# First batch of an attention and expert kernel: split loads, another order of jobs, and unread products in the pauses

## The chip, the cores and the metric

One core of a Trainium2 chip runs the program. The metric is the device time of one execution in microseconds (us). TensorE, VectorE, ScalarE, GpSimd and SyncE are the core's engines; they share the on-chip memory, and order between them comes from semaphores. TensorE's clock has two levels, 2.4 GHz (a granted clock of 1.00 in the tables) and 1.2 GHz (0.50).

## The reference

For 4 sequences of 1024 tokens of width 256: attention with 16 heads of 16, then a top-2 mixture of 8 experts, each followed by a residual and a layernorm.

```python
q = einsum('bsc,oc->bso', x, wq); k = ...wk; v = ...wv          # 16 heads of 16
q_embed = stack([softplus(q) * cos(pos), softplus(q) * sin(pos)])
k_embed = stack([softplus(k) * cos(pos + bias), softplus(k) * sin(pos + bias)])
attn = softmax(q_embed @ k_embed.T / 4); x = layernorm(x + (attn @ v) @ wo.T)
gates = softmax(x @ router_w + router_b); top 2, capacity 640 tokens an expert
h = gelu(rows_e @ w1[e] + b1[e]); out = h @ w2[e] + b2[e]
x = layernorm(x + sum over the chosen experts of gate * out)
```

## The kernel before, in words

The program has two launches in one: `attention`, then `experts`, with a turn between them at which the engines meet.

**Attention.** The work is cut into 16 groups (4 sequences, 4 groups of 4 heads), each of 16 steps; a step is one tile of 128 keys against 512 queries for 4 heads. TensorE makes a step's scores (`scores`, L828), ScalarE their exponentials (L621), and TensorE one step later the product with the values (`values`, L852). Queries and keys enter in two parts, a rounded one and its remainder, so that three products stand for one precise one.

Between the steps TensorE runs *jobs* from a table written by hand (`misc_schedule`). A job belongs to a step; negative steps are those before the attention of the first group. For batch 0, the first eight heads of the first sequence, they are four projections `qk` (query and key, first and second half of the sequence: units 0 to 3), four jobs of values `v`, `norms` (a bound on the scores, from squares) and `count`. The jobs before step 0 write to four PSUM banks in turn, `misc` and the first halves of the three score buffers (`banks`, `bank`), and a job waits until the bank that it takes has been read. TensorE waits at step 0 until all early jobs are read (`s_free`), for the first half of the stacks (`s_half`), and then reads a flag that `count` gives, to choose between two forms of the group (`choose`).

A projection's unit runs through the engines. ScalarE makes a softplus in three passes (`softplus`, L581 to L585). VectorE (`split_unit`) makes `raw` (L978), multiplies by the angles' cosines and sines into `emb` (L988) and rounds it (L994); GpSimd subtracts for the remainder (`split_rest`, L496). ScalarE squares `raw` for the norms (L590). SyncE stores both parts in DRAM (`store`, L330) and loads them back as stacks in the layout of the heads (`fill_half`, L369, half of the sequence each; `fill`, L384, for the next group). Step 4 of the first group waits for the second half. Each engine's own order is the order of its program: VectorE makes the keys' angles (`key_angles`) ahead of unit 0, and the constants (`set_up`, L958 to L966) between units 1 and 2.

**The turn.** After the last group VectorE finds the slots of the last tokens (L1175), GpSimd scatters their rows to the experts' buffers in DRAM (L511), and the launch ends. The second launch loads the rows (L1347), turns them on TensorE (L1403), and runs expert after expert: hidden layer L1423, output L1442.

## Time and profile before

| | |
|---|---|
| median of three runs | 1006.29 us (1005.87 to 1007.37) |
| the profiled execution, its own time | 1010.19 us |
| its span in the trace | 1008.4 us |
| TensorE busy (weight loads apart) | 907.8 us, 90% |
| weight loads | 518.8 us, 51% |
| VectorE, ScalarE, GpSimd busy | 631.4, 657.1, 362.0 us |

The trace gives every instruction's start and duration from the start of the span. An idle time stands before the instruction that ends it, with the operation that released it behind an arrow. An f32 product of TensorE is two records, so that a projection of two products counts x4 and a job of values x8.

### The profile page before, as it was taken

How to read it: one execution, taken by the hardware profiler on the slowest of the kernel's cores; microseconds unless marked ns; L12 is line 12 of the kernel's file. 1: busy time of each engine (PE TensorE's matmuls, PEld its weight loads, DVE VectorE, ACT ScalarE, POOL GpSimd, SP SyncE). 2: the span in 40 equal slices, each digit the busy share in tenths (PEclk: the TensorE clock that was granted, in tenths of full speed). 3: DMA queues.
4: the chain of work that ended last, by engine and by line, in shares of the span. 5: the costliest groups of instructions: out<-in, count | busy, mean ns of one | idle time of the engine just before them, and what ended most of it. 6: DMA issues, size and time to landing. Idle time of an engine off the chain costs nothing. (4 is left out here: it accounts for less than half of the span.)

```text
span 1008.4 us, 19281 instructions
## 1 busy us (share of the span) xinstructions
PE 907.8 (90%) x7597; PEld 518.8 (51%) x7597; DVE 631.4 (63%) x1109; ACT 657.1 (65%) x762; POOL 362.0 (36%) x271
## 2 busy tenths in 40 slices
PE   5599999999999999999999989999099999999950
PEld 2333343334344334444434434344089999999940
DVE  5467556647868465767564775437466777877626
ACT  4289888897778888867888777986134344444315
POOL 2137243433235654415545520233603333222332
PEclk9599999999999999999999999999589999999985
DMA  6728742333415343332542425231165544333245
GB/s 225 256 79 266 264 147 75 131 137 131 173 49 179 118 169 142 131 133 89 192 143 66 174 73 187 67 101 35 50 199 137 137 111 131 91 97 95 27 114 246
DMA packets 62133, 135.32 MB, mean 134 GB/s; under 512 B 8563, under 2 KB 33460, under 8 KB 60752
## 3 DMA queue, kind: packets, MB, share of 16 engines
q1 hardware_dynamic: 42848, 85.99, 25.6%
q0 software_dynamic: 19184, 47.99, 15.9%
q8 instruction: 62, 1.02, 0.4%
q14 instruction: 39, 0.32, 0.1%
HBM read 72.47 MB, written 61.95 MB: 133 GB/s over the span
## 5 line engine op out<-in xcount | busy, mean ns | idle before, releaser
L621 ACT ACTIVATE prob<-spsum 128x1024 f32<-128x1024 f32 x512 | 492.8, 1022 | 136.7 <-PE spsum L828 130.2
L852 PE MATMUL opsum<-prob,val 128*17 128x512 f32 x2048 | 270.5, 598 | 2.6 <-DVE oraw L1187 1.4
L828 PE MATMUL spsum<-area_q 32*128 32x512 f32 x1536 | 136.0, 429 | 4.7 <-issue 2.4
L828 PEld LDWEIGHTS spsum<-area_q 32*128 32x128 f32 x1536 | 75.4, 185 | 117.1 <-issue 72.5
L1380 POOL DMA_INDIRECT sum_scratch<-eo,add_idx x40 | 70.3, 1757 | 176.3 <-ACT eo L1483 169.2
L828 PE MATMUL spsum<-stacks 32*128 32x512 f32 x1536 | 132.0, 425 | 1.2 <-ACT prob L621 0.5
L828 PEld LDWEIGHTS spsum<-stacks 32*128 32x128 f32 x1536 | 72.4, 183 | 113.9 <-ACT prob L621 61.8
L494 POOL TENSOR_TENSOR square<-raw 128x512 bf16<-128x512 f32 x28 | 58.0, 2073 | 192.6 <-DVE raw L983 192.6
L1194 DVE RECIPROCAL oden<-oden 128x256 f32<-128x256 f32 x62 | 108.7, 1753 | 2.1
L496 POOL TENSOR_TENSOR area_s<-emb,area_s 128x1024 fp32r<-128x1024 f32 x32 | 76.0, 2376 | 41.9 <-DVE area_s L994 41.9
L537 POOL TENSOR_TENSOR onorm<-oraw,oden 128x512 f32<-128x512 f32 x31 | 42.2, 1361 | 131.7 <-DVE oden L1194 131.7
L1472 ACT ACTIVATE hraw<-hp,b 128x640 f32<-128x640 f32 x64 | 51.0, 797 | 56.5 <-PE hp L1423 56.5
L511 POOL DMA_INDIRECT dispatched<-res,scatter_idx x64 | 65.5, 1023 | 58.9 <-issue 25.1
L852 PEld LDWEIGHTS opsum<-prob,val 128*17 128x17 f32 x2048 | 36.4, 95 | 95.2 <-ACT prob L621 60.2
L1483 ACT ACTIVATE eo<-biased,gate 128x256 f32<-128x256 f32 x40 | 20.4, 510 | 88.9 <-DVE biased L1590 88.9
L1187 DVE COPY oraw<-opsum 128x512 f32<-128x512 f32 x31 | 21.4, 692 | 77.2 <-PE opsum L852 68.9
L665 PE MATMUL misc<-xT,wqkv 128*128 128x512 f32 x116 | 60.5, 646 | 8.0 <-DMA wqkv<-in_wk 7.4
L1442 PE MATMUL yp<-area_q,hid 128*128 128x256 f32 x480 | 61.1, 284 | 0.0
L1442 PE MATMUL yp<-w2s,hid 128*128 128x256 f32 x480 | 59.8, 282 | 0.0
L1423 PE MATMUL hp<-xe,area_s 128*128 128x320 f32 x384 | 59.3, 315 | 0.0
L1423 PEld LDWEIGHTS hp<-xe,area_s 128*128 128x128 f32 x384 | 58.6, 194 | 0.0
L1442 PEld LDWEIGHTS yp<-area_q,hid 128*128 128x128 f32 x480 | 57.8, 189 | 0.1
(198 smaller groups left out, 1075.5 us busy)
## 6 DMA issues: line engine op xcount, KB each, us to landing
split_scratch<-area_s POOLq DMA_DIRECT2D x56, 512.0 KB, 4.1
area_k<-in_w SPq DMA_DIRECT2D x16, 1024.0 KB, 5.8
stacks<-split_scratch SPq DMA_DIRECT2D x28, 512.0 KB, 5.5
area_q<-split_scratch SPq DMA_DIRECT2D x28, 512.0 KB, 5.4
dispatched<-blank POOLq DMA_DIRECT2D x1, 5300.0 KB, 25.7
rows<-dispatched SPq DMA_DIRECT2D x7, 662.5 KB, 4.6
xT<-in_xT SPq DMA_DIRECT2D x4, 1024.0 KB, 6.6
res<-in_x SPq DMA_DIRECT2D x4, 1024.0 KB, 8.4
```

The lines of the kernel that those rows point to most:

```text
L494: pool.tensor_tensor(square[:, i], raw[:], raw[:], ALU.mult).then_inc(s_square, 1)
L496: pool.tensor_tensor(split[u % 2][:, 1], embs[u % 2][:], split[u % 2][:, 0].bitcast(F32), ALU.subtract).then_inc(s_split, 1)
L511: pool.indirect_dma_start(disp_d, bass.IndirectOffsetOnAxis(ap=scatter_idx[:, k, t:t + 1], axis=0), ress[UNITS[u][0] % 2][:, t, :], None, ...
L621: act.activation(prob[u % NPB][:], spsum[u % NSB][:].rearrange("p a n -> p (a n)"), ACT.Exp, scale=HD ** -0.5).then_inc(s_exp, 1)
L665: ins = pe.matmul(misc[:], wqkv[:, qk, k, P * ct:P * (ct + 1)], xT[:, k, HALF * half:HALF * (half + 1)], start=k == 0, stop=k == KC - 1)
L828: ins = pe.matmul(spsum[u % NSB][:, j % 2, :], kst[par][rows, a, P * kt:P * (kt + 1)], qst[par][rows, b, cols], start=i == 0, stop=i == 2 ...
L852: ins = pe.matmul(opsum[32 * j:32 * j + HD + 1, :], val[b % 2][:, kt, h0 + j, :], prob[(2 * s + j // 2) % NPB][:, HALF * (j % 2):HALF * (j ...
L1194: tell(dve.reciprocal(half, half), s_sums)
L1380: pool.indirect_dma_start(sum_d, bass.IndirectOffsetOnAxis(ap=add_idx[e % 2][:, t:t + 1], axis=0), eo[e % 2][:, t, :], None, bounds_check= ...
L1423: ins = pe.matmul(hp[n % 2][:, h, 0:CH], w1s[e % 2][:, b, k, P * m:P * (m + 1)], xe[e % 2][:, a, k, CH * h:CH * (h + 1)], start=k == 0 and ...
L1442: ins = pe.matmul(yp[n % 2][:, 0:DIM], hids[:, a, m, P * t:P * (t + 1)], w2s[e % 2][:, b, m, :], start=m == 0 and i == 0, stop=m == HK - 1 ...
L1472: act.activation(hraw[n % NH][:].rearrange("p (h n) -> p h n", h=2), hp[n % 2][:, :, 0:CH], ACT.Gelu, bias=b1[:, e, m:m + 1]).then_inc(s_g ...
```

## The change

It touches the first batch, and adds products in pauses of TensorE.

- The loads of x and of the query angles come in halves, each with a semaphore; the constants come in another order, `blank` later.
- The early jobs are ordered qk, v, norms, count, and use seven banks in place of four.
- `raw` of units 2 and 3 goes to the buffers `oden` and `onorm`. VectorE makes the remainders of batch 0 itself; GpSimd doesn't take part in batch 0's units, and sets up the constants.
- The keys' angles are made for the first half only at first. For the second half ScalarE makes the first products, and VectorE adds the second (`late_angles`), around the readouts of norms and count. The values are copied by ScalarE (`first_values`), which also rounds units 2 and 3.
- `idle_products`: products of a constant with itself, 128x128, to a bank that nobody reads afterwards: 14 at the start; 14 when two squares are there and 4 when three are, ahead of the norms; 12 ahead of step 0; 36 when the last slots are known; 8 at the start of the second launch.

```diff
-        put(-14 + i, ("qk", 0, i))
-        put((-8, -7, -4, -3)[i], ("v", 0, i))
+        put(-10 + i, ("qk", 0, i))
+        put(-6 + i, ("v", 0, i))
         put((1, 5, 9, 13)[i], ("qk", 1, i))
-    put(-6, ("norms", 0))
-    put(-5, ("count", 0))
+    put(-2, ("norms", 0))
+    put(-1, ("count", 0))
...
-        banks = [misc, *(b[:, 0, :] for b in spsum)]
+        banks = [misc, *(b[:, n, :] for b in spsum for n in range(2))]
...
-            sp.dma_start(wqkv[:, 0], wq_d).then_inc(s_wqk, 16)
-            sp.dma_start(xT, xT_d[0]).then_inc(s_xT, 16)
-            sp.dma_start(wqkv[:, 1], wk_d).then_inc(s_wqk, 16)
-            sp.dma_start(qtrig, trig_d).then_inc(s_trig, 16)
-            sp.dma_start(blank[:], blank_d).then_inc(s_blank, 16)
+            sp.dma_start(wqkv[:, 0], wq_d).then_inc(s_wqk[0], 16)
+            sp.dma_start(xT[:, :, 0:HALF], xT_d[0][:, :, 0:HALF]).then_inc(s_xfirst[0], 16)
+            sp.dma_start(wqkv[:, 1], wk_d).then_inc(s_wqk[1], 16)
+            sp.dma_start(qtrig[:, :, 0:HALF], trig_d[:, :, 0:HALF]).then_inc(s_trig[0], 16)
+            sp.dma_start(xT[:, :, HALF:], xT_d[0][:, :, HALF:]).then_inc(s_xfirst[1], 16)
+            sp.dma_start(qtrig[:, :, HALF:], trig_d[:, :, HALF:]).then_inc(s_trig[1], 16)
             sp.dma_start(wqkv[:, 2], wv_d).then_inc(s_wv, 16)
+            sp.dma_start(tri_f[:], tri_d).then_inc(s_const, 16)
+            sp.dma_start(blocks_f[:], blocks_d).then_inc(s_const, 16)
+            sp.dma_start(ident[:], ident_d).then_inc(s_const, 16)
             sp.dma_start(woT[:, :, 0:DIM], wo_d).then_inc(s_const, 16)
...
+            sp.dma_start(blank[:], blank_d).then_inc(s_blank, 16)
...
+            for i in range(2):
+                pool.memset(val[i][:, :, :, HD:HD + 1], 1.0)
+            pool.memset(ones[:], 1.0)
+            pool.memset(before[:], 0.0)
+            pool.memset(unit[:], 0.0).then_inc(s_clear, 1)
+            pool.wait_ge(s_clear, 1)
+            pool.wait_ge(s_const, 16 * NCONST)
+            pool.tensor_copy(tri[:], tri_f[:])
+            for k in range(KC):
+                pool.tensor_copy(unit[:, k, P * k:P * (k + 1)], ident[:])
+            pool.tensor_copy(blocks[:], blocks_f[:]).then_inc(s_setup, 1)
...
+            def first_batch():
+
+                softplus(0)
+                softplus(1)
+                first_square(0)
+                softplus(2)
+                first_square(1)
+                softplus(3)
+                first_values(0)
+                first_square(2)
+                first_square(3)
+                act.wait_ge(s_trig[1], 16)
+                for t in range(2):
+                    act.mul(ktrig[:, 0, t, HALF:], qtrig[:, 1 - t, HALF:], ang[:, (3, 5)[t], 0:1]).then_inc(s_late, 1)
+                for i in range(1, 4):
+                    first_values(i)
+                for u in (2, 3):
+                    act.wait_ge(s_emb, u - 1)
+                    for v in (u - 2,):
+                        stored(act, 0, v)
+                    act.copy(split[u % 2][:, 0], embs[u % 2][:]).then_inc(s_hi, 1)
...
                     pe.wait_ge(s_setup, 1)
+                    if c == 0:
+                        for u, count in ((2, 14), (3, 4)):
+                            pe.wait_ge(s_square, u)
+                            idle_products(pe, misc[:, 0:P], ident, count)
                     pe.wait_ge(s_square, 4 * c + 4)
...
+            pe.wait_ge(s_krow, 1)
+            idle_products(pe, spsum[2][:, 1, 0:P], row_ones[:].bitcast(F32), 14)
             for s in range(first, last + 1):
                 if s == 0:
 
+                    idle_products(pe, bank(("norms", 0))[:, 0:P], ident, 12)
                     pe.wait_ge(s_free, early)
...
+            pe.wait_ge(s_idx, 2 * len(UNITS))
+            idle_products(pe, spsum[1][:, 0, 0:P], ident, 36)
             pe.br("attention_done")
...
+            def first_product(u):
+
+                qk, half = u % 2, u // 2
+                table = ktrig[:, 0] if qk else qtrig
+                tell(dve.tensor_tensor(embs[u % 2][:], raw_of(u)[:].unsqueeze(1).to_broadcast((P, 2, HALF)),
+                                       table[:, :, HALF * half:HALF * (half + 1)], ALU.mult), s_emb)
+
+            def first_rest(u):
+
+                dve.wait_ge(s_hi, u + 1)
+                counts[s_hi.name] = u + 1
+                tell(dve.tensor_tensor(split[u % 2][:, 1], embs[u % 2][:], split[u % 2][:, 0].bitcast(F32),
+                                       ALU.subtract), s_split)
+
+            def late_angles(t):
+
+                dve.wait_ge(s_late, t + 1)
+                link(dve.scalar_tensor_tensor(ktrig[:, 0, t, HALF:], qtrig[:, t, HALF:], ang[:, 4, 0:1],
+                                              ktrig[:, 0, t, HALF:], ALU.mult, ALU.add))
+
+            def first_split(u):
+
+                split_parts(0, u)
+                tell(dve.tensor_tensor(split[u % 2][:, 1], embs[u % 2][:], split[u % 2][:, 0].bitcast(F32),
+                                       ALU.subtract), s_split)
+
+            def first_batch():
+
+                dve.wait_ge(s_trig[0], 16)
+                key_angles(0, slice(0, HALF))
+                for u in (0, 1):
+                    first_raw(u)
+                    first_split(u)
+                for u in (2, 3):
+                    first_raw(u)
+                dve.wait_ge(s_trig[1], 16)
+                first_product(2)
+                read_out(("norms", 0))
+                late_angles(0)
+                read_out(("count", 0))
+                dve.wait_ge(s_vcopy, 4)
+                dve.sem_inc(s_free, 4)
+                counts[s_free.name] += 4
+                late_angles(1)
+                first_product(3)
+                for u in (2, 3):
+                    first_rest(u)
+                dve.wait_ge(s_setup, 1)
...
+def idle_products(pe, bank, square, count):
+
+    for _ in range(count):
+        pe.matmul(bank, square[:], square[:], start=True, stop=True)
...
+            idle_products(pe, yp[1][:, 0:P], ident, 8)
```

TensorE's program at its start, before (spsum and misc are the banks; square, tops: norms and count):

```order
L665 MATMUL misc<-xT,wqkv 128x512 x2
L665 MATMUL spsum<-xT,wqkv 128x512 x6
L674 MATMUL misc<-wqkv,xT 128x256 x4
L674 MATMUL spsum<-wqkv,xT 128x256 x4
L681 MATMUL spsum<-square,blocks 32x512 x4
L686 MATMUL spsum<-ident,tops 1x128
L674 MATMUL misc<-wqkv,xT 128x256 x4
L674 MATMUL spsum<-wqkv,xT 128x256 x4
```

And in the changed kernel (L1348 are the unread products):

```order
L1348 MATMUL spsum<-row_ones 128x128 x14
L716 MATMUL misc<-xT,wqkv 128x512 x2
L716 MATMUL spsum<-xT,wqkv 128x512 x6
L725 MATMUL spsum<-wqkv,xT 128x256 x12
L725 MATMUL misc<-wqkv,xT 128x256 x4
L1348 MATMUL spsum<-ident 128x128 x18
L736 MATMUL spsum<-square,blocks 32x512 x4
L741 MATMUL spsum<-ident,tops 1x128
L1348 MATMUL spsum<-ident 128x128 x12
```

All four value jobs stand ahead of the norms, and unread products stand in three places.

VectorE's program in the first batch, from the product of unit 1 on, before (area_s: rounded part, or with emb as input the remainder; oden, onorm: raw of units 2 and 3 in the change; area_k: the keys' angles):

```order
L988 TENSOR_TENSOR emb<-raw,area_k 128x1024
L994 CAST area_s<-emb 128x1024
...
L978 SCALAR_TENSOR_TENSOR raw<-spsum,soft 128x512
L988 TENSOR_TENSOR emb<-raw,qtrig 128x1024
L994 CAST area_s<-emb 128x1024
L978 SCALAR_TENSOR_TENSOR raw<-spsum,soft 128x512
L988 TENSOR_TENSOR emb<-raw,area_k 128x1024
L994 CAST area_s<-emb 128x1024
L1012 COPY val<-misc 128x32x16
L1012 COPY val<-spsum 128x32x16
L1015 TENSOR_REDUCE tops<-spsum 128x1
```

And in the changed kernel:

```order
L1086 TENSOR_TENSOR emb<-raw,area_k 128x1024
L1092 CAST area_s<-emb 128x1024
L1043 TENSOR_TENSOR area_s<-emb,area_s 128x1024
L1015 SCALAR_TENSOR_TENSOR oden<-spsum,soft 128x512
L1015 SCALAR_TENSOR_TENSOR onorm<-spsum,soft 128x512
L1024 TENSOR_TENSOR emb<-oden,qtrig 128x1024
L1111 TENSOR_REDUCE tops<-spsum 128x1
L1112 MEMSET pairs 1x128
L1037 SCALAR_TENSOR_TENSOR area_k<-qtrig,ang,area_k 128x512
...
L1037 SCALAR_TENSOR_TENSOR area_k<-qtrig,ang,area_k 128x512
L1024 TENSOR_TENSOR emb<-onorm,area_k 128x1024
L1031 TENSOR_TENSOR area_s<-emb,area_s 128x1024 x2
```

The constants and the copies of values have left; four remainders and two halves of the angles have come, and the second product of each pair stands behind the readouts of norms and count.

## Rows read from the trace of the kernel before

**Rows 1.** The page, part 2: granted TensorE clock in 40 slices of 25.2 us.
```profile
PEclk9599999999999999999999999999589999999985
```

**Rows 2.** The chain of waits, in order of time: start, us, what.
```profile
735.44 16.20 PE hp L1423 x96
...
766.90 14.07 PE hp L1423 x96
```

**Rows 3.** Timeline, TensorE: start, us, operation, count of records, idle before.
```profile
7.43 3.78 PE L665 MATMUL misc<-xT,wqkv 128*128 128x512 f32 x4 [7.43 <-DMA wqkv<-in_wk]
...
18.87 1.89 PE L674 MATMUL spsum<-wqkv,xT 128*128 128x256 f32 x8
...
35.04 3.78 PE L674 MATMUL misc<-wqkv,xT 128*128 128x256 f32 x8
...
38.62 2.73 PE L674 MATMUL spsum<-wqkv,xT 128*128 128x256 f32 x8
...
43.75 2.07 PE L828 MATMUL spsum<-area_q 32*128 32x512 f32 x14 [2.40 <-issue]
...
56.16 0.97 PE L828 MATMUL spsum<-area_q 32*128 32x512 f32 x12
...
59.15 1.98 PE L665 MATMUL misc<-xT,wqkv 128*128 128x512 f32 x4
```

**Rows 4.** Timeline, VectorE, first 45 us.
```profile
15.44 1.23 DVE L988 TENSOR_TENSOR emb<-raw,qtrig 128x1024 f32<-128x1024 f32 x1
...
16.70 0.69 DVE L994 CAST area_s<-emb 128x1024 fp32r<-128x1024 f32 x1
...
18.26 2.73 DVE L988 TENSOR_TENSOR emb<-raw,area_k 128x1024 f32<-128x1024 f32 x1
...
36.20 0.14 DVE L1023 TENSOR_SCALAR flags<-pairs 1x1 int32<-1x1 f32 x1
...
41.86 0.69 DVE L1012 COPY val<-spsum 128x512 f32<-128x512 f32 x1 [2.24 <-PE spsum L674]
```

**Rows 5.** Timeline, ScalarE, one pass of the first softplus.
```profile
11.87 0.63 ACT L584 ACTIVATE soft<-soft 128x512 f32<-128x512 f32 x1
```

**Rows 6.** Timeline, GpSimd, remainders of units 0, 1 and 3.
```profile
17.55 2.36 POOL L496 TENSOR_TENSOR area_s<-emb,area_s 128x1024 fp32r<-128x1024 f32 x1 [16.60 <-DVE area_s L994]
...
21.86 2.35 POOL L496 TENSOR_TENSOR area_s<-emb,area_s 128x1024 fp32r<-128x1024 f32 x1 [1.95 <-DVE area_s L994]
...
32.35 2.34 POOL L496 TENSOR_TENSOR area_s<-emb,area_s 128x1024 fp32r<-128x1024 f32 x1 [1.95 <-DVE area_s L994]
```

**Rows 7.** SyncE's loads of the stacks, and landing of loads into area_q.
```profile
28.79 1.76 SPq L369 DMA_DIRECT2D area_q<-split_scratch  x4
...
41.28 1.75 SPq L369 DMA_DIRECT2D area_q<-split_scratch  x4
...
DMA to landing us min/median/max: 2.8/3.9/6.0
```

**Rows 8.** Windows of half a us; the column 1.00 to 0.50 is the granted clock.
```profile
23.00:23.50 0.50, 0.00 (x0) 0.00 (x0) 0.47 (x1) 0.00 (x0) 0.50 (x1) 0.73 1.03 389
...
40.00:40.50 0.50, 0.50 (x3) 0.42 (x2) 0.00 (x0) 0.00 (x0) 0.00 (x0) 0.70 0.40 156
...
43.50:44.00 0.50, 0.25 (x4) 0.28 (x8) 0.00 (x0) 0.00 (x0) 0.00 (x0) 0.71 0.75 262
```

**Rows 9.** Timeline, TensorE, products of 8 columns with f32 weights.
```profile
275.23 1.06 PE L732 MATMUL misc<-wr,x1T 128*128 128x8 f32 x8
```

**Rows 10.** Timelines at the turn of the launches: VectorE, GpSimd, ScalarE, TensorE.
```profile
715.23 0.19 DVE L1175 TENSOR_REDUCE scatter_idx<-rt 128x4 int32<-128x32 f32 x1
...
726.49 0.97 POOL L511 DMA_INDIRECT dispatched<-res,scatter_idx  x1 [0.30 <-issue]
...
729.17 1.28 ACT L1463 ACT_TABLE_LOAD   x1 [17.61 <-PEq L159]
...
731.30 1.25 PE L1403 MATMUL tp<-ident,rows 128*128 128x128 f32 x4 [18.17 <-DMA rows<-dispatched]
```

More of the change, by code:

```diff
@@ L273, in jobs_at, with raw_of @@
             return jobs.get(s, ())
+        def raw_of(u):
+            return (oden, onorm)[u - 2] if u in (2, 3) else raws[u % 2]
         def softplus_at(s):
@@ L490, in split_rest @@
                 pool.wait_ge(s_raw, u + 1)
-                if c:
-                    pool.wait_ge(s_full, number["norms", c - 1] + 1)
-                if c:
-                    pool.tensor_tensor(square[:, i], raw[:], raw[:], ALU.mult).then_inc(s_square, 1)
+                pool.wait_ge(s_full, number["norms", c - 1] + 1)
+                pool.tensor_tensor(square[:, i], raw[:], raw[:], ALU.mult).then_inc(s_square, 1)
                 pool.wait_ge(s_hi, u + 1)
@@ L537, in normalise @@
                 pool.tensor_tensor(onorm[:], oraw[:], oden[:], ALU.mult).then_inc(s_norm, 1)
-            for s in range(first, last + 1):
+            for s in range(last + 1):
                 for u in splits_at(s):
@@ L589, in first_square, with first_values @@
                 act.wait_ge(s_raw, u + 1)
-                act.activation(square[:, u], raws[u % 2][:], ACT.Square).then_inc(s_square, 1)
+                act.activation(square[:, u], raw_of(u)[:], ACT.Square).then_inc(s_square, 1)
+            def first_values(i):
+                act.wait_ge(s_full, number["v", 0, i] + 1)
+                act.wait_ge(s_clear, 1)
+                act.copy(val[0][:, 2 * i:2 * i + 2, :, 0:HD],
+                         bank(("v", 0, i))[:].rearrange("p (t h d) -> p t h d", t=2, h=HEADS)).then_inc(s_vcopy, 1)
+            def first_batch():
[18 more added lines that the diff above has]
+                    act.copy(split[u % 2][:, 0], embs[u % 2][:]).then_inc(s_hi, 1)
             def rstd_guess(u):
@@ L612, in gates_exp @@
                 act.activation(rt[:, 0, t0:t1], rt[:, 1, t0:t1], ACT.Exp).then_inc(s_gexp, 1)
-            for s in range(first, last + 1):
-                if 0 <= s < NSTEP:
+            first_batch()
+            for s in range(last + 1):
+                if s < NSTEP:
                     for u in (2 * s, 2 * s + 1):
@@ L654, in begin, with x_loaded @@
                     pe.wait_ge(s_free, n - len(banks) + 1)
+            def x_loaded(b, half):
+                if b:
+                    pe.wait_ge(s_xT, 16 * b)
+                else:
+                    pe.wait_ge(s_xfirst[half], 16)
             def run(job):
@@ L955, in set_up @@
-            def set_up():
-                for i in range(2):
-                    link(dve.memset(val[i][:, :, :, HD:HD + 1], 1.0))
-                link(dve.memset(ones[:], 1.0))
-                link(dve.memset(before[:], 0.0))
-                link(dve.memset(unit[:], 0.0))
-                dve.wait_ge(s_const, 16 * NCONST)
-                link(dve.tensor_copy(tri[:], tri_f[:]))
-                for k in range(KC):
-                    link(dve.tensor_copy(unit[:, k, P * k:P * (k + 1)], ident[:]))
-                tell(dve.tensor_copy(blocks[:], blocks_f[:]), s_setup)
+            dve.wait_ge(s_sin, 1)
@@ L968, in split_unit @@
             def split_unit(c, i):
-                ct, qk, half = c % KC, i % 2, i // 2
                 u = 4 * c + i
@@ L1211, in general_maxima @@
                     dve.sem_inc(g_free, GEN + 2)
-            for s in range(first, last + 1):
+            first_batch()
+            for s in range(last + 1):
                 if 0 < s < NSTEP and s % TB == 0:
@@ L1227, in _ @@
                     split_unit(u // 4, u % 4)
-                if s == first + 1:
-                    key_angles(0)
-                if s == first + 3:
-                    set_up()
                 if s == 3:
-                    key_angles(1)
+                    key_angles(1, slice(0, SEQ))
                 for part in range(2):
```

67 lines of the change are left out of this document (30 added, 37 removed).

## The prediction

> **What bounds the kernel now.** I read the page first. TensorE is busy nearly throughout, and its granted clock is low in the second slice (25 to 50 us), in the 29th and 30th (706 to 756), and at the very end [rows 1]. The chain of waits that ended last runs through the second launch on TensorE; its first expert takes 16.20 us where the next takes 14.07 [rows 2]. So the middle of the run is a dense TensorE stream whose steps have no date of their own, and a time saved ahead of it should reach the end whole. What can be saved lies in the first 60 us and around 705 to 740.
>
> TensorE's order of time [rows 3] shows the start: projections from 7.43, a hole with only the norms in it, value products from 35.04 at half rate, the first attention product at 43.75, step 4 at 56.16, and a projection for the next batch of heads, in step 5, at 59.15. VectorE [rows 4] shows why: the flag that chooses the group's form is ready at 36.34, but the last copy of values ends at 42.55, and TensorE waits for all early banks to be free. The queue of the loads [rows 7] shows a second date: the second half of the stacks is asked for at 41.28, lands in time for step 4, and costs nothing now. Two facts are needed from the windows [rows 8]: the clock falls to 1.2 GHz about 2.5 us after TensorE stops (work ended at 20.8, fall in the slice at 23.0; ended at 41.4, fall in the slice at 43.5), and comes back to 2.4 about 5.3 us after steady work began (35.04 to 40.3).
>
> **The change, part by part.** Costs are from rows; sums are against the profiled execution's own 1010.19 us (span 1008.4). It stands 3.90 above the median of the three runs, 1006.29, so the gain is taken off both.
>
> *Unread products.* Their shape, 128x128 in f32 with weights loaded each time, is not in the trace. A product has two records. The nearest rows: eight records of 128x8 f32, weights 128x128, take 1.06 us with their drain, 0.12 to 0.13 each [rows 9]; a 128x512 f32 product has two records of about 0.5 warm (1.98 for four), a quarter of the columns giving 0.12. So 0.24 us warm, 0.48 cold; bounds 0.21 and 0.30 warm. Fourteen from about 1.0: 5.3 us cold (11 products), 3 warm: end 7.0. Projection of the first queries could begin when its weights and half of x are there, earlier than 7.43, but TensorE is held until 7.0. Gain of the split load: 0.4 us only; what the products give is the clock: four projections at 1.75, where the first took 3.78 [rows 3].
>
> *Projections and values.* Four at 1.75 from 7.0 end at 14.0; four value jobs at 1.75 (1.89 with its drain, the row at 18.87) end at 21.0. They need seven banks, now there.
>
> *ScalarE and VectorE in the batch.* Softplus of a unit is three passes of 0.63 plus gaps, 1.95 [rows 5]. The first projection is drained at 8.9, so the first softplus ends at 8.9 + 1.95 = 10.85. VectorE then takes, per unit, raw 0.69 (as the copy of this size at 41.86), gap 0.15, product 1.23, cast 0.69 [rows 4], and now the remainder, 1.23 as a product of that shape, with gaps 4.1 us. GpSimd's remainder took 2.36 and blocked a VectorE product meanwhile: 2.73 instead of 1.23 for the one at 18.26, begun while GpSimd ran until 19.91 [rows 4, 6]. Two units end at 10.9 + 8.1 = 19.0 (before: 24.21). The two raws 20.6, product of unit 2 21.95. GpSimd has the constants off VectorE's queue (2.7 us there). The Trainium skill ("SBUF — State Buffer", Who interferes with whom) says that a VectorE instruction with two SBUF inputs contends with a GpSimd one that reads SBUF, one blocking the other; that rule agrees with the 2.73, and speaks against the constants' copies on GpSimd at about 14.6. By it unit 1 would be up to 1.5 us later, and the first attention product too, but not the norms or step 4.
>
> *Stores and the first half.* Before, unit 1 was ready at 24.21 and the first half was asked for at 28.79, 4.6 later; the last of four loads is issued 1.3 after, landing took 2.8 to 6.0 [rows 6, 7]. Now: 19.0 + 4.6 = 23.6, landed near 30 (28.8 to 30.9).
>
> *Norms.* TensorE is free at 21.0, yet 14 + 4 unread products stand ahead of the norms: 18 x 0.24 = 4.3, norms out at 25.7, though their last square is ready at about 21.3. So the products that keep the clock cost 4 us here of whatever hangs on the norms, and on VectorE everything behind the readout does: tops 0.7, late angle 0.7, count 1.1: flag at 28.6; late angle, product of unit 3 (1.23), two remainders: 33.0. The twelve further products end at 30, about when the half is landed; the branch took 1.2 (42.55 to 43.75). First attention product at 31.2, against 43.75: 12.5 us earlier.
>
> *What is late next.* Step 4 needs the second half. Unit 3's remainder was ready at 34.69 and the loads issued at 41.28, 6.6 later with two stores back to back. Now 33.0 + 6.6 = 39.6; 4.6 if the stores did not queue, 37.6. Last landing another 5.2 to 7.3 after; I take 6.2, nearer the slow end because the next group's loads follow directly, as before. Step 4 at 45.8 instead of 56.16: 10.4 earlier. TensorE gets there about 40.4 (steps 0 to 3 and one projection, warm, with ScalarE's exponentials of 1.0 setting steps 0 and 1) and stands about 5.4 us. Both shorter pauses above lost the clock, so it comes back cold for 5.3 us, half of which, 2.6, is lost; the eight value records of 35.04 took 3.78 where those of 18.87 took 1.89, and a cold stretch does half the work. Net at step 5: 7.8 us.
>
> *Before the experts.* The indices are ready at 715.42, the last scatter's issue ends at 727.5 and the next launch starts at 729.17 [rows 10]. Thirty-six products from there: 5.3 us cold are 11, the other 25 at 0.24 are 6.0: end 726.7, hidden behind the scatters. The cover, 12.1 us, is gone only above 0.34 us a product on the mean. The pause to 729.2 is 2.5 us, just about what has lost the clock; eight more products there, 1.9 warm, end at 731.1 while rows land at 731.3. Warm, expert 0 takes 14.07 instead of 16.20, 2.1; the transposes ahead are bound by VectorE and give 0.5. Gain 2.6, bounds -1.7 (eight cold products, 3.8, after which work starts 1.7 late) and 3.1.
>
> *The rest.* Two more loads and the order of the constants: their issue, 0.43 a load (1.75 for four) [rows 7], is on SP's queue, which is ahead of every need. Zero.
>
> Sum: 7.8 + 2.6 = 10.4. Own time 999.8; median 1006.29 - 10.4 = 995.9.
>
> **The rivals.**
> - *A: little or no pause at step 4.* If stores do not queue and land in 5.2, step 4 is at 42.8, TensorE stands 2.4 us and may keep the clock. For: the second set of stores queued behind loads before, and no longer does. Against: two stores of 1 MB back to back move at what one already fills. Gain 13.4 to 15.6 + 2.6: median 988 to 990.3. Chance 0.23.
> - *B: the clock is lost before the experts.* The pause there, 2.5 us, equals what lost it twice [rows 8]. Then eight cold products delay the first transpose by 1.7, but shorten the cold part of expert 0: net about 0.4. Median 1006.29 - 8.2 = 998.1. The Trainium skill ("TensorE: Matmul & The Clock Gate", What's actually happening) says the monitor's window runs freely, so the same kernel can change clock at different points. By that rule, A and B could differ from run to run. Chance 0.17.
> - *C: slower.* The place is the 36 products. They stand ahead of TensorE's part in the end of the first launch, which without them goes by the scatters, 727.5. If they never bring the clock back and cost more than planned, that end moves and expert 0 gains nothing. It turns to a loss when they end past 727.5 + 7.8 = 735.3, that is at over 19.9 / 36 = 0.55 us each. At 0.65 they end at 738.8, 11.3 late, and the median is 1006.29 - 7.8 + 11.3 = 1009.8. For: shape unseen. Against: cold value products with twice the columns take 0.95 each (3.78 for four) [rows 3]. Chance 0.03.
> - *D: the change does less than it says in the batch.* VectorE's longer row of work, or loads in halves that land later, put step 4 at 51, 5.2 earlier than before; less the cold stretch and with the experts, 5.2 - 2.6 + 2.6: median 1001.1. For: the squares and both raws all hang on one engine. Against: durations are all from rows. Chance 0.07.
>
> **How the numbers follow.** Main case 0.50: median 995.9; landing 1 us either way and products of 0.21 to 0.30 take it from 993.5 to 998. A reaches 988, B 998.1, D 1001.1. Range 988.3 to 1000.5, leaving out D, C and a corner of A. A measurement tells about 0.2%, 2.0 us, from no change. Faster by over that: 0.95; within: 0.02; slower: 0.03.
>
> **What would show it.** Right: the first projection near 7, four at 1.75; 18 products between value products and norms with a VectorE hole before the tops; first attention product near 31; a TensorE pause ahead of step 4 that ends with the landing of the stacks; granted clock 2.4 GHz when expert 0 starts, and 14.1 us for it [rows 2]. Wrong: no pause at step 4, norms that wait for squares instead of products, a first launch whose end waits for TensorE, or expert 0 at 16.

## The result, and the profile after

| | before | after |
|---|---|---|
| median of 7 runs each, us | 1006.29 (1005.34 to 1008.44) | 1003.34 (1001.44 to 1003.96) |
| ratio, 95% interval | | 0.9955 [0.9940, 0.9969] |
| profiled execution: own time, span | 1010.19, 1008.4 | 1003.59, 1001.7 |
| granted clock, mean | 0.957 | 0.968 |

The change is faster, by 4.5 us going by the ratio (3.1 to 6.0 by its interval; the medians differ by 2.95), where 10.4 were forecast. Its median of 1003.34 lies above the range (988.3 to 1000.5).

The page, part 2, as [rows 1], in slices of 25 us: the clock of the second slice has gone from 0.5 to 0.8, that of the 29th from 0.5 to 0.7, and that of the 30th from 0.8 to 0.9 (0.90 in the window 725 to 750).

```profile
PEclk9899999999999999999999999999799999999985
```

TensorE's timeline of the first 60 us answers to [rows 3].

```profile
1.00 5.84 PE L1348 MATMUL spsum<-row_ones 128*128 128x128 f32 x28 [1.00 <-POOL row_ones L482]
7.42 1.96 PE L716 MATMUL misc<-xT,wqkv 128*128 128x512 f32 x4 [0.58 <-DMA xT<-in_xT]
...
19.54 1.89 PE L725 MATMUL misc<-wqkv,xT 128*128 128x256 f32 x8
21.27 4.18 PE L1348 MATMUL spsum<-ident 128*128 128x128 f32 x36
25.38 0.41 PE L736 MATMUL spsum<-square,blocks 128*32 128x512 bf16 x4
...
31.79 1.19 PE L883 MATMUL spsum<-area_q 32*128 32x512 f32 x14 [1.77 <-issue]
33.86 1.64 PE L883 MATMUL spsum<-area_q 32*128 32x512 f32 x10 [0.88 <-ACT prob L668]
35.43 3.78 PE L716 MATMUL misc<-xT,wqkv 128*128 128x512 f32 x4
...
43.67 1.05 PE L907 MATMUL opsum<-prob,val 128*17 128x512 f32 x8
48.09 1.65 PE L883 MATMUL spsum<-area_q 32*128 32x512 f32 x12 [3.36 <-issue]
...
53.09 2.40 PE L716 MATMUL misc<-xT,wqkv 128*128 128x512 f32 x4
```

The first projection is no earlier than before. The wait that ended there was another one: the weights of the keys before, as [rows 3] has it (`wqkv<-in_wk`), and the first half of x now. The 18 products (36 records) stand ahead of the norms, and step 4 starts after a pause of 3.36 us. VectorE's timeline (beside [rows 4]) shows its hole behind those products, and SP's (beside [rows 7]) the date at which the second half is asked for.

```profile
11.98 0.69 DVE L1015 SCALAR_TENSOR_TENSOR raw<-misc,soft 128x512 f32<-128x512 f32 x1
...
18.89 1.23 DVE L1043 TENSOR_TENSOR area_s<-emb,area_s 128x1024 fp32r<-128x1024 f32 x1
...
21.82 1.23 DVE L1024 TENSOR_TENSOR emb<-oden,qtrig 128x1024 f32<-128x1024 f32 x1
25.92 0.69 DVE L1111 TENSOR_REDUCE tops<-spsum 128x1 f32<-128x512 f32 x1 [2.87 <-PE spsum L736]
...
31.03 2.48 DVE L1031 TENSOR_TENSOR area_s<-emb,area_s 128x1024 fp32r<-128x1024 f32 x2
```
```profile
25.23 1.76 SPq L378 DMA_DIRECT2D area_q<-split_scratch  x4
32.33 3.42 SPq L337 DMA_DIRECT2D split_scratch<-area_s  x4
40.38 1.75 SPq L378 DMA_DIRECT2D area_q<-split_scratch  x4
```

The windows (as [rows 8]; the granted clock stands after POOL's busy time) show that the clock is lost twice in here, ahead of the projection at 35.43 and in the pause ahead of step 4.

```profile
33.00:36.00 3.00, 2.14 (x11) 1.33 (x12) 0.52 (x1) 2.58 (x3) 0.00 (x0) 0.58 0.85 313
36.00:39.00 3.00, 3.00 (x4) 0.67 (x2) 0.00 (x0) 1.07 (x2) 0.00 (x0) 0.50 1.02 378
...
45.00:48.00 3.00, 0.00 (x0) 0.00 (x0) 0.00 (x0) 0.50 (x1) 0.00 (x0) 0.85 0.95 255
48.00:51.00 3.00, 2.91 (x20) 1.05 (x20) 0.00 (x0) 1.23 (x2) 0.00 (x0) 0.50 0.97 399
```

At the turn, TensorE's timeline and the last scatter on GpSimd's (beside [rows 10]):

```profile
708.39 10.36 PE L1348 MATMUL spsum<-ident 128*128 128x128 f32 x72 [2.34 <-DVE scatter_idx L1271]
723.56 3.37 PE L1348 MATMUL yp<-ident 128*128 128x128 f32 x16 [4.81 <-PEq L159]
726.76 0.60 PE L1502 MATMUL tp<-ident,rows 128*128 128x128 f32 x4
...
730.09 15.73 PE L1523 MATMUL hp<-xe,area_s 128*128 128x320 f32 x96
```
```profile
719.49 0.98 POOL L528 DMA_INDIRECT dispatched<-res,scatter_idx  x1 [0.31 <-issue]
```

The chain of waits gives the two experts of [rows 2] as they are now:

```profile
730.44 15.38 PE hp L1523 x96
...
760.90 14.08 PE hp L1523 x96
```

The 36 products are hidden, as planned: they end at 718.7, before the last scatter. But TensorE then pauses for 4.8 us, not 2.5; the clock is lost, the eight products run cold (3.37), and expert 0 is still slow.

**Where the time lies.** The attention drains its output once every block of eight steps, with one VectorE copy (`oraw`). Its first and its 31st start cut a span into four pieces, with the end of expert 0's 96 records as the third cut. These are the first and last of 31 rows of after, then of before:

```profile
62.48 0.69 DVE L1283 COPY oraw<-opsum 128x512 f32<-128x512 f32 x1 [2.06 <-PE opsum L907]
...
670.29 0.69 DVE L1283 COPY oraw<-opsum 128x512 f32<-128x512 f32 x1 [1.20 <-PE opsum L907]
```
```profile
68.13 0.69 DVE L1187 COPY oraw<-opsum 128x512 f32<-128x512 f32 x1 [2.06 <-PE opsum L852]
...
677.34 0.69 DVE L1187 COPY oraw<-opsum 128x512 f32<-128x512 f32 x1 [1.57 <-PE opsum L852]
```

The same for every profiled execution of this study, in us (chips differ: e1 to e4 ran on one, e5 to e8 and e9 to e12 on two others):

| run | start to block 1 | to block 31 | to expert 0's end | to the end | span |
|---|---|---|---|---|---|
| before | 68.1 | 609.2 | 74.3 | 256.8 | 1008.4 |
| after | 62.5 | 607.8 | 75.5 | 255.9 | 1001.7 |
| e1_none | 58.3 | 614.4 | 76.3 | 256.6 | 1005.5 |
| e2_behind | 59.9 | 615.6 | 77.4 | 256.4 | 1009.3 |
| e3_no_norm_products | 58.1 | 617.5 | 80.1 | 256.4 | 1012.2 |
| e4_before_look | 66.8 | 614.0 | 77.3 | 256.8 | 1014.9 |
| e5_after_again | 61.8 | 607.8 | 76.8 | 256.2 | 1002.6 |
| e6_vector_order | 57.8 | 607.6 | 76.0 | 256.7 | 998.1 |
| e7_combo | 56.5 | 608.4 | 73.7 | 256.6 | 995.3 |
| e8_bridge | 61.8 | 608.0 | 73.5 | 255.9 | 999.2 |
| e9_no_turn | 59.5 | 608.5 | 73.9 | 256.0 | 997.8 |
| e10_order_bridge | 58.0 | 607.3 | 73.5 | 256.0 | 994.8 |
| e11_order_no_start | 59.2 | 607.9 | 72.3 | 256.5 | 995.9 |
| e12_loads_whole | 58.6 | 608.8 | 73.8 | 256.2 | 997.4 |

So the change gained 5.6 us in the start and 1.4 in the middle, lost 1.2 at the turn, and 0.9 came at the end: 6.7 between the two profiled executions. Each row is one execution. Five of them have the change's own order up to step 4 (after, e2, e5, e8, e9), and their starts lie between 59.5 and 62.5, so a difference of 2 us between two starts can be chance.

### The profile page after: what moved, and what is told of

It reads as the page before. It is cut to its first block and busy times, and to the rows that moved or that the text cites. A ratio compares the mean times of both kernels' runs of the same rounds, so it can differ in the third digit from the quotient of the medians.

```text
span 1001.7 us, 19639 instructions
## 1 busy us (share of the span) xinstructions
PE 928.0 (93%) x7773; PEld 540.4 (54%) x7773; DVE 628.1 (63%) x1100; ACT 662.1 (66%) x770; POOL 355.8 (36%) x276
## 5 line engine op out<-in xcount | busy, mean ns | idle before, releaser
L512 POOL TENSOR_TENSOR square<-raw 128x512 bf16<-128x512 f32 x28 | 58.1, 2074 | 204.4 <-DVE raw L1074 204.4
L514 POOL TENSOR_TENSOR area_s<-emb,area_s 128x1024 fp32r<-128x1024 f32 x28 | 66.7, 2382 | 17.6 <-DVE area_s L1092 17.6
L1283 DVE COPY oraw<-opsum 128x512 f32<-128x512 f32 x31 | 21.4, 692 | 74.7 <-PE opsum L907 66.4
L1523 PEld LDWEIGHTS hp<-xe,area_s 128*128 128x128 f32 x384 | 57.8, 192 | 0.0
```

The costliest lines, as they stand in the source:

```text
L512: pool.tensor_tensor(square[:, i], raw[:], raw[:], ALU.mult).then_inc(s_square, 1)
L514: pool.tensor_tensor(split[u % 2][:, 1], embs[u % 2][:], split[u % 2][:, 0].bitcast(F32), ALU.subtract).then_inc(s_split, 1)
L1523: ins = pe.matmul(hp[n % 2][:, h, 0:CH], w1s[e % 2][:, b, k, P * m:P * (m + 1)], xe[e % 2][:, a, k, CH * h:CH * (h + 1)], start=k == 0 and ...
```

## The experiments

Two theories stood against each other: that the unread products pay with the clock, as the prediction had it, and that they hold up as much as they give. The first four kernels ran on a chip on which the kernel before took 1016.03 us.

**No unread product at all.** `idle_products` goes at all five places (14, 14 + 4, 12, 36, 8).

> The changed kernel without any of its 74+8 unread products. Theory 1 (what hangs on the norms sets the second half of the stacks and so step 4; the products at the turn hold back the end of the first launch): the first projection still starts near 7.4, now cold, so the value products end near 24 instead of 21.4; the norms follow at once at about 24.5 instead of 25.4, step 4 starts at about 47 instead of 48.1. The next launch starts about 1.7 us after the last scatter is issued instead of 3.0, and its first transposes about 2.4 us earlier relative to the attention, with expert 0 cold at 16.2 instead of 15.4. In all 1 to 3 us faster than the changed kernel (ratio to before 0.993 to 0.995). Theory 2 (the products are worth their clock): 3 us or more slower than the changed kernel, ratio to before 0.998 or above.

Measured: 1007.88 us, ratio to before 0.9914 [0.9888, 0.9941]. No slower than the change (0.9955 and, below, 0.9946, on other chips; the change itself wasn't run on this one), and further below the kernel before than the 0.993 to 0.995 of theory 1. Theory 2 falls. Step 4 comes at 46.31 without a pause, the launch 1.74 us after the last scatter, and expert 0's records take 16.2 us, cold, as expected.

**The 36 products behind TensorE's branch.**

```diff
-            pe.wait_ge(s_idx, 2 * len(UNITS))
-            idle_products(pe, spsum[1][:, 0, 0:P], ident, 36)
             pe.br("attention_done")
 ...
             nc.switch_bb("attention_done")
+            pe.wait_ge(s_idx, 2 * len(UNITS))
+            idle_products(pe, spsum[1][:, 0, 0:P], ident, 36)
```

> The 36 products stand behind TensorE's branch to the last block instead of ahead of it. Theory 1 (the 4.8 us between the last product and the next launch are TensorE fetching code behind its branch, and the launch waits for it): the pause shrinks to 2 to 3 us, the next launch starts 1.7 us after the last scatter's issue instead of 3.0, the clock may still be at 2.4 GHz at the transposes and expert 0 takes 14.1 to 14.5; 1.3 to 3.5 us faster than the changed kernel. Theory 2 (the 4.8 us are the engines' meeting at the end of a launch): nothing moves, the pause stays 4.8 us and the time is the same within 1 us.

Measured: 1009.99 us, 0.9927 [0.9905, 0.9949]. TensorE's timeline at the turn:

```profile
718.52 10.37 PE L1348 MATMUL spsum<-ident 128*128 128x128 f32 x72 [3.79 <-issue]
730.91 2.02 PE L1348 MATMUL yp<-ident 128*128 128x128 f32 x16 [2.01 <-PEq L159]
```

The pause is 2.0 instead of 4.8, the launch comes 1.7 us after the last scatter, and the eight products are warm, so theory 2 falls. But the clock was lost again during the transposes (0.59 from 736 to 739), and expert 0's records took 15.4 us, not 14.1 to 14.5. The turn as a whole, 77.4, is as long as that of the kernel before on this chip (77.3, e4), and the interval overlaps those of the change. So this run shows what moved the launch, not a gain at the turn.

The view of the DMA queues shows a reason: a queue of kind "instruction" moves two packets (name, packets, MB, share). In the change, 708.4 to 716 has none and 716 to 723.5 has these:

```profile
q0 software_dynamic: 215, 0.17, 7.6%
q8 instruction: 2, 0.03, 1.9%
```

In e10 below, which has the products behind the branch, 701 to 707 has them, and 707 to 717.1 none:

```profile
q0 software_dynamic: 144, 0.15, 8.1%
q8 instruction: 2, 0.03, 2.4%
```

The dates of the packets fit one reading: the code behind the branch is brought only as TensorE gets near it. Where the 36 stand ahead of the branch (after, e3, e5, e6, e12), the first packet starts 1.2 us before they end, and the second 3.1 to 3.6 us after the first. In the change the second ends at 722.00, 1.5 us after the last scatter (720.47), and the launch's first record on ScalarE starts at 723.51. From the end of the second packet to that record it is 1.51 or 1.52 us in after, e3, e5 and e6, while the last scatter ended 2.5 to 3.3 us before it. In every other kernel here both packets are there before the last scatter ends, or are not awaited (e12, below), and that distance from the scatter is 1.71 or 1.72. That the packets hold this code is read from the queue's name and from these dates; no experiment changed the code's size or place alone.

**No products ahead of the norms** (without the 14 and 4).

> The changed kernel without the 14 + 4 products ahead of the norms. Theory 1: the norms start when the last square is there, 22.4 instead of 25.4, the flag is ready at 25.8 instead of 28.8, unit 3's remainder at 30.6 instead of 33.5, step 4 at 45.1 instead of 48.1: 3 us faster than the changed kernel. Theory 2 (without them the clock falls at about 24 and the first steps run cold): first steps cold anyway in both, step 4 waits for the stacks, so at most 1 us of the 3 comes back; if the gain is below 1 us, theory 1's gate is wrong.

Measured: 1009.43 us, 0.9919 [0.9898, 0.9941]. Norms at 23.14, step 4 at 46.14 with no pause, block 1 at 58.1; but the first attention product came at 33.16, not earlier, since it waits for the first half (asked 25.32), and the first steps were cold. Theory 1 had step 4 at 45.1. The profiled execution, 1014.03 us, is the slowest of its six and 4.6 above their median, so its row of the table is longer than usual by about that much.

**The kernel before, traced on this chip.**

> The kernel before once more, with its trace. Theory 1 (the profiled execution used for the forecast was slow by chance, 1010.19 against a median of 1006.29, and its cold stretches were longer than usual): this one comes in near 1006 and shows by the clock's windows or the waits where 3 to 4 us went. Theory 2 (the profiler's executions always take longer): again near 1010.

Measured: 1016.66 us. This chip's execution is 6.5 us longer in span than the first. The middle has 4.8 of it: blocks 15, 16, 23 and 24 took 21.08, 20.99, 21.07 and 20.96 us, where 19.93, 19.98, 19.91 and 20.00 stand in the first trace of before. It stands only 0.6 above this chip's median of before (1016.03), where the first trace stood 3.9 above its own. So theory 2 falls: a profiled execution isn't always 4 us longer, and the first one was probably slow by chance. The start took 68.1 us there and takes 66.8 here.

The next four ran together on another chip (before: 1007.54 us).

**The change again.**

> The change as it is, unchanged, on the same chip as the three kernels sent with it. If what the run without any unread product showed is general (theory: the unread products pay nothing in sum), this one stands about 4 to 6 us below the kernel before, as in the first comparison (1003.34 to 1006.29), and its launch of the expert stage comes 2.5 to 3.1 us after the end of the last scatter's issue. If the difference between runs was the chip's (rival), the gain against the kernel before comes out at 8 us or more here.

Measured: 1002.43 us (998.74 to 1006.56, 8 runs), 0.9946 [0.9924, 0.9968]. The gain is the same as at first on this second chip, so the rival falls here. The chip of e1 to e4 never ran the change.

**Another order on VectorE.** The late products and remainders go ahead of the readouts that wait for TensorE.

```diff
                 first_product(2)
-                read_out(("norms", 0))
                 late_angles(0)
-                read_out(("count", 0))
-                dve.wait_ge(s_vcopy, 4)
-                dve.sem_inc(s_free, 4)
-                counts[s_free.name] += 4
                 late_angles(1)
                 first_product(3)
                 for u in (2, 3):
                     first_rest(u)
+                read_out(("norms", 0))
+                read_out(("count", 0))
+                dve.wait_ge(s_vcopy, 4)
+                dve.sem_inc(s_free, 4)
+                counts[s_free.name] += 4
```

> VectorE takes the late products, the late angles and both remainders ahead of the two readouts that wait for TensorE's 18 unread products. Theory (the 2.9 us wait in VectorE's queue sets when the first half is handed over): the last remainder ends about 30 instead of 33.5, the next projections are asked about 36.5 to 37.5 instead of 40.4, step 4 starts about 43.5 instead of 48.1, and the end comes 2 to 4 us before that of the change. First rival (the first half's landing gates step 0 anyway, and the pause moves there): the flag comes about 3 us later than 28.8, the first attention product starts 34 or later, and the gain against the change is under 1 us. Second rival: slower than the change, because the flag that GpSimd's late indices wait for comes late.

Measured: 998.07 us, 0.9902 [0.9883, 0.9920]: 4.4 us below the change. SP's queue and TensorE's timeline:

```profile
27.87 3.85 SPq L337 DMA_DIRECT2D split_scratch<-area_s  x4
37.86 1.75 SPq L378 DMA_DIRECT2D area_q<-split_scratch  x4
```
```profile
29.93 0.59 PE L741 MATMUL spsum<-ident,tops 128*1 128x128 f32 x2 [3.72 <-DVE tops L1111]
30.44 5.49 PE L1348 MATMUL spsum<-ident 128*128 128x128 f32 x24
35.86 1.33 PE L883 MATMUL spsum<-area_q 32*128 32x512 f32 x14
...
44.87 1.05 PE L907 MATMUL opsum<-prob,val 128*17 128x512 f32 x8
45.85 0.97 PE L883 MATMUL spsum<-area_q 32*128 32x512 f32 x12
...
47.74 1.15 PE L883 MATMUL spsum<-area_q 32*128 32x512 f32 x12
```

The second half is asked for 3.5 us sooner than in e5 (37.86, 41.32). The first attention product comes 2.0 later (35.86, 33.84), as the first rival had it, and yet the gain isn't under 1 us: step 4 starts at 45.85 (43.5 was expected) with no pause ahead of it, and the clock stays. Block 1 is 4.0 us earlier than in e5, of 4.5 between the two spans.

**Several edits together:** e6's order; no products ahead of the norms, 24 behind them, 5 ahead of step 0; the turn as in e8.

> No unread products ahead of the norms, 24 behind them, 5 ahead of step 0, the late values ahead of the readouts on VectorE, the 36 products behind TensorE's branch, and two after each of the first four transposes. Theory: step 4 without a pause (about 43 to 44), launch of the expert stage 1.7 to 2.0 us after the scatter, clock full through the transposes, expert 0 in 14.1 to 14.6 us instead of 15.4; 5 to 7 us below the change. Rival (the clock is lost in the first steps again, and the attention's blocks give back what their start gained): expert 0 as expected, but the end only 2 to 3 us below the change.

Measured: 997.11 us, 0.9900 [0.9879, 0.9921], 5.3 below the change; step 4 at 44.54 without a pause, and block 1 is the earliest of all, at 56.5. The turn took 73.7, as in e8 and e10, though TensorE waited 1.75 us in it for gathered rows. Against e6 the medians differ by 1.0, and the intervals overlap.

**The turn mended:** the 36 behind the branch, and two products behind each of the first four transposes.

```diff
             for t in range(ST):
                 turn(0, t)
+                if t < ST - 1:
+                    idle_products(pe, yp[1][:, 0:P], ident, 2)
```

> The change with the 36 products behind TensorE's branch, and two unread products after each of the first four transposes of the turn. Theory (two separate costs at the turn: the code behind the branch fetched after the products, about 1 us, and the clock lost during the transposes, about 1.3 us): the launch comes 1.7 to 2.0 us after the scatter's end, the clock stays full, expert 0 takes 14.1 to 14.4 us, and the whole is 2 to 3 us below the change. Rival (the transposes wait for the gathered rows, and products between them add time): expert 0 starts 0.5 to 1 us later, and the whole is within 1.5 us of the change.

Measured: 1000.36 us, 0.9928 [0.9910, 0.9946]: 2.1 below the change, start unchanged (block 1 at 61.8). Last scatter to launch 1.8 us; expert 0's records take 14.8 us from first to last, where the change has 15.7 (after) and 16.6 (e5), and the turn 73.5. The two edits weren't run apart on this chip.

The last four ran together (before: 1008.25 us).

**No products at the turn** (without the 36 and the eight).

> The change without the 36 and the eight unread products of the turn; its start is untouched. Theory (the turn's 44 products gain nothing: the launch is held back by what they keep from being fetched, and the clock is lost anyway): the launch of the expert stage 1.7 us after the last scatter instead of 2.7 to 3.0, expert 0 in 15.4 to 16.3 us, and the whole within 1 us of the change. Rival (they pay, as the prediction had it, 2.6 us): 2 us or more slower than the change.

Measured: 1000.56 us, 0.9931 [0.9915, 0.9946]; not slower than the change, so the turn's 44 products gained nothing as they were placed. The turn took 73.9 us, with 75.5 and 76.8 in the change. The rival falls. Nor is it slower than e8: 0.9931 beside 0.9928, and a turn of 73.9 beside 73.5. So even where they are placed well, the turn's unread products are worth 0.4 us in the traces, which is within what one execution differs from another. This execution also showed how sharp the edge at step 4 is. Its start is the change's, yet step 4 came at 47.53 after 2.42 us, and the clock did not fall. One window each, of e5 and of e9:

```profile
48.00:51.00 3.00, 2.49 (x20) 0.89 (x20) 0.00 (x0) 1.02 (x2) 0.00 (x0) 0.63 1.01 404
```
```profile
48.00:51.00 3.00, 3.00 (x32) 1.20 (x26) 0.00 (x0) 2.47 (x3) 0.00 (x0) 1.00 1.04 421
```

Step 4 was 0.98 us earlier than in e5, block 1 2.3 earlier. The 0.8 of it that the second half was asked for sooner (40.51, 41.32) agree with the loads at the start: TensorE waited 0.70 us for x's second half at 11, in e5 1.41.

**Both mends together.**

> VectorE's new order and the mended turn together (36 products behind the branch, two behind each of the first four transposes). If the two are separate costs, as their places in the program say, the gains add: the fifth step without a pause (block 1 read at about 57.8), expert 0 in 14.6 us, and 994.5 to 997 us beside 1002.4 of the change and 998.1 and 1000.4 of the two apart. Rival (the turn's pause grows with what the attention gains, for instance because GpSimd's scatters become the last to arrive): no better than 998.

Measured: 996.81 us (995.53 to 998.26), 0.9891 [0.9875, 0.9906]. With e7 and e11 the fastest here, and faster than both kernels of this case. TensorE's timeline:

```profile
717.19 2.02 PE L1348 MATMUL yp<-ident 128*128 128x128 f32 x16 [2.25 <-PEq L159]
719.84 0.44 PE L1502 MATMUL tp<-ident,rows 128*128 128x128 f32 x2 [0.63 <-DMA rows<-dispatched]
...
723.99 1.13 PE L1525 MATMUL hp<-xe,area_s 128*128 128x320 f32 x6
725.31 13.47 PE L1525 MATMUL hp<-xe,area_s 128*128 128x320 f32 x90 [0.19 <-DVE xe L1631]
```

By the ratios the gains against the change are 4.4 (e6), 1.8 (e8) and 5.5 (both): nearly a sum. Not run was e6's order with no unread product anywhere, which by e9 and e11 could be as fast.

**The same without the 14, 18 and 12 products of the start.**

> The same, without the 14, 18 and 12 unread products of the start: what these are worth once VectorE's queue is free of the wait. Theory (their price was VectorE's wait; what is left is the clock of the first projections and first steps): first projections 3.75 us for four instead of 1.95, the norms' products about 24, the clock reached later in the first steps, block 1 read at 58.3 to 59.5, 0.5 to 2 us slower than with them. Rival (first and second half's landing set the steps, not the clock): the same within 0.5 us.

Measured: 997.68 us, 0.9894 [0.9879, 0.9910], block 1 at 59.2 against 58.0. With the order mended they are worth 1.2 us of the start in the traces and 0.9 in the medians, with intervals that overlap, so that isn't shown to be more than nothing.

**Loads whole.** `xT` and `qtrig` come in one load each again, in the places of their first halves.

> The change with x and the angle table loaded whole again, nothing else. Theory (the split gained nothing, since the half of x lands as late as the whole did, 7.4 us): the first projection starts 6.5 to 7.5, without the wait of 0.3 to 1.6 us for x's second half at 10 to 12; VectorE's first angle operations start up to 3 us later than 9.4, and the whole is within 1 us of the change. Rival (the half table is what lets VectorE start, and everything behind it follows): the remainder of unit 3 ends 1.5 us or more later than 33.5, and the whole is 1.5 us or more slower.

Measured: 1001.00 us, 0.9935 [0.9919, 0.9952]; not slower than the change. The first projection started at 6.85, and the wait of 0.3 to 1.6 us for x's second half at 10 to 12 was gone. The DMA view says why the split gained nothing (KB each, us to landing), after, then before:

```profile
xT<-in_xT SPq DMA_DIRECT2D x2, 512.0 KB, 6.3
```
```profile
xT<-in_xT SPq DMA_DIRECT2D x1, 1024.0 KB, 5.0
```

The 6.3 is the middle of 5.6 for the first half and 7.0 for the second. Half the bytes took no less time from issue to landing: the first half landed at 7.28 in after and between 6.1 and 7.1 in e5 to e11, the whole at 6.69 in before and at 6.71 here. What the split did was to put the second half off, to 10.6 in after and 10.8 to 11.6 in e5 to e11. That many loads in flight share the way would explain it, but isn't shown. VectorE's table was little helped: its first half landed at 9.27 in after (10.29 in e5), the whole at 9.90 here.

At the turn, the launch came 1.7 us after the last scatter though the 36 products stand ahead of the branch. Here the second packet ended at 719.95, after the launch's first record (719.29), so this launch didn't wait for it. Why it could do without isn't shown; a program of another length may have its code cut into packets at another place. So the late code cost 0.8 us (e3) to 1.6 (e6) in four of the five executions that have the 36 ahead of the branch (after, e3, e5, e6, e12).

## Why the prediction was wrong

- **Unread products, 0.24 us warm:** right (4.18 / 18 = 0.23). Fourteen end at 6.8 (7.0 forecast), projections at 14.4 (14.0), values at 21.4 (21.0).
- **Split load, 0.4 gained:** wrong. The half of x landed at 7.28, the whole before it at 6.69. The projection at 7.43 before had waited for the keys' weights, not for x. In e5 to e10 the first projection began at 6.4 to 7.3, with whole loads (e12) at 6.85; and in those six the second half made TensorE wait again, for 0.3 to 1.6 us.
- **ScalarE and VectorE in the batch, two units by 19.0:** 20.1. The forecast let VectorE start on `raw` when the first softplus was ready. It had first to make the angles, four operations that waited for the table's landing at 9.36, and took `raw` at 11.98. By the Trainium skill ("SBUF — State Buffer", Who interferes with whom) GpSimd's constant copies could have held unit 1 up. They ran from 15.80 to 16.90. VectorE's remainder of unit 0, with two SBUF inputs, had 0.2 us left then and took its usual 1.23; `raw` at 16.06 reads one input from PSUM, and by the same section wouldn't contend; the next product began at 16.90. So nothing was held up, and the rule wasn't tested.
- **First half asked at 23.6, flag 28.6, last remainder 33.0, first attention product 31.2:** 25.2, 28.8, 33.5, 31.8. Right in order, up to 1.6 late. (The forecast's earliest landing of the first half, 28.8, uses the median of 3.9 us; with the shortest, 2.8, it is 27.7.) Left out was that the clock fell again just behind the first product, in the waits for the first exponentials; the projection at 35.43 took 3.78. TensorE had to wait at step 4 anyway, so this was probably hidden; no run separates it. The forecast took from two stretches that the clock falls 2.5 us after TensorE stops and is back 5.3 us after work begins. As a rule it doesn't hold: pauses of 1.88 and 1.90 us lost it (e2, e5), though work was back sooner than 2.5 us, and one of 2.42 kept it (e9).
- **Second half asked at 39.6, landed 6.2 later, step 4 at 45.8, net 7.8 at step 5:** asked at 40.4, step 4 7.7 later at 48.1; the next batch's projection came 6.1 earlier (59.15, now 53.09). The mechanism was right, with clock loss and all; its size was 1.7 too large. Step 4 came 2.3 later than forecast, 0.8 of it by the request and 1.5 by the landing; the cold stretch behind it cost 2.0 instead of 2.6. What the prediction saw and did not price as avoidable was its own line on the norms: that 18 products "cost 4 us here of whatever hangs on the norms". That wait in VectorE's queue was worth 4.4 us of the whole (e6), as much as the entire change gained.
- **The turn, 2.6 gained:** this is the step that failed most: 1.2 lost, 3.8 off. With those 3.8 us the median of 1003.34 would have been 999.5, within the range. What the forecast had wrong is the wait behind the 36 products: it took the launch to go by the scatters alone, with a pause of 2.5 us. Rival B had the clock lost, with 0.4 us gained all the same; the traces have 1.2 to 2.5 us lost. The 36 products cost nothing by their own time, as forecast, but the launch came 3.0 us after the last scatter instead of 1.7: by the dates of the packets they put off the fetch of the code behind the branch, which the sum did not contain. The pause was 4.8 instead of the 2.5 forecast, the eight products ran cold ahead of the transposes (3.4 us), and expert 0's records got back 0.8 us at most (16.55, now 15.73 and 16.64). Behind the branch, and with the transposes bridged, the turn is 2.0 to 3.3 us shorter than the change's (e8, e10), and 0.8 shorter than before's. Rival C named the right place for a loss, the 36 products ahead of the launch's end, with the wrong price.
- **The sum:** 10.4 forecast; 6.7 between the profiled executions, 4.5 by the ratio. From 10.4 to 6.7 it is 2.2 too much in the start and 3.8 at the turn, less 1.4 and 0.9 that came in the middle and at the end and that nobody forecast: that much was luck. The last 2.2 are mostly because the profiled execution of before stood 3.90 above its median, and that of after at its own; a difference of traces overstates the gain here. The forecast took its gain off both, the trace and the median, and gave no reason why a slow execution should lose as much as a usual one. In what part of the first trace those 3.9 us lie isn't shown.
- **Rival A** (no pause at step 4) did not come, but it was the better design: e6 had no pause at step 4, with 10.3 us gained in the start, not the 13.4 to 15.6 of the rival.

## What to carry to other kernels

Work that only keeps an engine busy is not free when another engine's queue has a wait on what comes behind it: take that engine's independent work ahead of the wait first, and only then ask whether the filler still pays (here it was 4.4 us for the order, and for the filler 0.9 at the start and 0.4 at the turn, neither clear of chance). Don't put filler ahead of a branch to code that is needed soon; put it behind. And cut the traces at fixed marks into pieces before believing one total: a gain of 5.6 in one piece hid a loss of 1.2 in another.

## What the runs showed of the hardware

- Code behind a branch can come late. Two packets on the "instruction" queue come near TensorE's branch at the turn, and where the 36 products stood ahead of it, the launch began 1.51 or 1.52 us after the second packet's end (after, e3, e5, e6), which is 0.8 to 1.6 us later than by the scatter; in e12 it didn't wait for it.
- Ahead of step 4, pauses of 1.97 (e12) and 2.42 us (e9) kept the clock; those of 1.88 (e2), 1.90 (e5) and 3.36 (after) lost it (0.67, 0.63 and 0.50 in windows of 3 us behind). So the length of the pause alone did not decide. Executions of one kernel lie up to 7.8 us apart (998.74 to 1006.56, e5). The Trainium skill ("TensorE: Matmul & The Clock Gate", What's actually happening) has the monitor's window run freely; e5 and e9, with one code on TensorE up to here, agree with it, though their own dates differ by up to 1 us as well, which could be the reason too.
- Filler does not always raise the clock by itself: in e6 the products of 30.44 ran at half rate to the end (5.49 us for 12), and the work behind them had it (0.50 from 30 to 36, 0.97 from 36 to 39).
- One chip took 1.0 to 1.2 us longer in the same four of the 31 blocks (15, 16, 23 and 24), in before and in e1 to e3 alike.
